# A three-sublayer decoder block: expert weights split in advance through a ring, base experts by groups of tiles, the step loop written out, and a causal zeroing on GpSimd

## The chip, the cores and the metric

The kernel runs on one core of one Trainium2 chip. The metric is the device time of one execution in microseconds (us), lower is better. Three timed runs of the kernel before gave 732.4, 735.15 and 735.88 us.

## The reference, cut to what matters

There are 16 sequences of 128 tokens with 256 features. Each sublayer adds its input and normalizes the rows afterwards.

```python
x = layernorm(x + self_attention(x))        # 16 heads of 16, one shared K/V head, causal, softmax
x = layernorm(x + cross_attention(x, ctx))  # 32 query heads on 8 K/V heads of 8, softmax
# mixture: a base expert for all tokens, and 2 of 8 experts (256 -> 2*512 -> 256) for each token
probs = softmax(x @ gate_w); w, idx = top_k(probs, 2); w = w / w.sum()
y = silu_mul(x @ base_gate_up) @ base_down
  + sum_e comb[:, e] * (silu_mul(x @ expert_gate_up[e]) @ expert_down[e])
x = layernorm(x + y)
```

All inputs and outputs are float32.

## The kernel before

There are two stages. The attention stage handles one sequence (one tile of 128 rows) per step in a software pipeline of 22 steps. Each engine has an order written by hand (`PE_ORDER`, `ACT_ORDER`, `DVE_ORDER`, `POOL_ORDER`, `SP_ORDER`); an entry such as `("s_main", 0, 2)` means that in step s the engine does unit 0 of that stage for tile s + 2. An engine runs its order strictly from left to right, and semaphores tie the engines together. Eight of the 22 steps run as two passes of a loop with four steps in its body (`run`), the others are written out.

In self-attention, scores are computed twice: with queries on partitions for the row maximum (`s_max`), and with keys on partitions, the maximum subtracted (`s_main`), for the exponential. ScalarE takes the exponential (`s_exp`, L438), and `s_sum` multiplies the weights with V and with ones. The causal mask is added by TensorE as a bf16 product with the identity, ahead of both score products:

```python
pe.matmul(scores[:, n, at:at + 512], ident_b[:], mask_kq[:], start=True, stop=False)      # L784
mm = pe.matmul(scores[:, n, at:at + 512], k_s[p][:, b, :], q_s[p][:, 4 * bank:4 * bank + 4, :], start=False, stop=True)
```

Score results go through a ring of two PSUM slots, smaller ones through the ring `misc` of two banks, exponentials through four slots of `prob`. Products that need the accuracy of float32 are written in the attention stage as three products of FP32R parts (`three`, L722: high times high, high times low, low times high). Float32 products in the expert stage are single instructions for the programmer, and stand in the trace as two records each.

The expert stage begins when the attention stage has ended. TensorE transposes the 16 tiles (L1251), computes the router logits (L1258), and then works through 55 jobs: 10 tiles of the base expert, 39 tiles of rows sorted by expert, and 6 base tiles. While the first base jobs run, VectorE works out which row goes where (`shift_logits` to `slot_rows`), and GpSimd then gathers rows by indirect DMA three jobs ahead. A job is two halves of inner products (512 columns each, L1299), four transposes of the hidden tile (`turn_hidden`, L1306), two transposes of a later job's rows (`turn_rows`, L1313) and the outer product (L1322). Before the first half of a sorted job the sequencer of TensorE waits for the turned rows, and then reads the expert's number from memory (`value_load`, L1292). All weights of the eight experts lie in SBUF. Each result tile is copied out and scattered to HBM. During the last base jobs the chosen results come back, and VectorE adds them with their shares (`add_shares`, L1182 and L1185), then the last normalization follows.

Of the kernel before, what the change touches and what calls it, by code (L numbers as in the profile page):

```python
# [7 lines left out]
F32 = mybir.dt.float32  # L8
F32R = mybir.dt.float32r
# [16 lines left out]
CONST_COLS = 3 * P + 22  # L26
# [7 lines left out]
BASE_FIRST = 10  # L34
AHEAD = 3
ROUTE_COLS = 2 * P + SLOTS + EXPERTS * EXPERTS + PICKS + 1 + EXPERTS
# [15 lines left out]
    ("s_shift", 0, 3), ("c_main", 3, 0), ("s_out", 1, 2), ("c_max", 1, 1), ("c_sum", 0, 0),  # L52
]
# [5 lines left out]
    ("c_exp", 3, 0), ("s_rows", 0, 4),  # L59
# [11 lines left out]
    ("s_split", 0, 4), ("c_keys", 0, 1), ("x_bias", 0, 2),  # L71
]
SP_ORDER = [
    ("load_xT", 0, 4), ("load_ctx", 0, 2), ("load_base", 0, 2), ("load_x", 0, 2),
]
# [22 lines left out]
    "c_out": [("c_ctx", 2, None)],  # L98
}
# [81 lines left out]
def decoder_layer(nc, x, xT, ctx, ctxT, wqkvT, bqkv, woT, bo, gate_w, base_gu, base_down, exp_gu, exp_down, consts,  # L181
                  routing, out):
    x2 = nc.dram_tensor("x2", (B * S, D), F32, kind="Internal").ap()
    shared = nc.dram_tensor("chosen_y", (CHOICES * B * S, D), F32, kind="Internal").ap()
    with ExitStack() as both:
# [6 lines left out]
        base_up, base_dn = sb("base_up", [P, 2, 2 * INNER]), sb("base_dn", [P, INNER // P, D])  # L192
        ident = sb("ident", [P, P])
        eps = sb("eps", [P, 1])
        gate = sb("gate", [P, 2, EXPERTS])
        base_loaded = both.enter_context(nc.semaphore("base_loaded"))
        attention(nc, x, xT, ctx, ctxT, wqkvT, bqkv, woT, bo, consts, stream, ident, eps, base_gu, base_down,
                  gate_w, gate, base_up, base_dn, base_loaded)
        experts(nc, exp_gu, exp_down, routing, x2, shared, stream, ident, eps, gate, base_up, base_dn, base_loaded, out)


def attention(nc, x, xT, ctx, ctxT, wqkvT, bqkv, woT, bo, consts, stream, ident, eps, base_gu, base_down,
              gate_w, gate, base_up, base_dn, base_loaded):
    score_ring, prob_ring, sum_ring, misc_ring = rings()
    with ExitStack() as scope:
# [3 lines left out]
        def two(name, shape, dt=F32):  # L209
# [10 lines left out]
        mask_qk, mask_kq = sb("mask_qk", [P, 4, P], BF16), sb("mask_kq", [P, 4, P], BF16)  # L220
        blk_s, blk_c = cst[:, 3 * P:3 * P + 2], cst[:, 3 * P + 2:3 * P + 6]
        neg_s, neg_c = cst[0:32, 3 * P + 6:3 * P + 14], cst[0:32, 3 * P + 14:3 * P + 22]
# [43 lines left out]
        names = """consts_loaded weights_loaded w_hi w_split wo_split tables values_set  # L266
            xT_hi_set xT_split x_biased s_qkv_full s_qkv_read s_rows_hi s_rows_lo s_q_full s_q_read s_k_full s_k_read
            s_max_full s_max_read s_shift_full s_shift_read s_main_full s_exp s_summed s_sum_read
            s_out_full s_den_set s_ctx s_ctx_full s_ctx_hi s_ctx_read s_res_full s_res_read s_stats s_mv s_ln s_rsqrt0
# [8 lines left out]

        wo_loaded = scope.enter_context(nc.semaphore("wo_loaded"))
# [4 lines left out]
        def run(eng, order, stages):  # L284
# [6 lines left out]
            for s in range(FIRST_STEP, LOOP_FROM):  # L291
                step(s)
            with eng.Fori(0, LOOP_STEPS // UNROLL) as i:
                for u in range(UNROLL):
                    step(LOOP_FROM + u, i)
            for s in range(LOOP_FROM + LOOP_STEPS, LAST_STEP + 1):
                step(s)
# [9 lines left out]
        def _(sp):  # L307
# [28 lines left out]
            def load_base(seq, unit):  # L336
                if seq.i is None and seq.off == 0:
                    sp.dma_start(base_up[:], base_gu.rearrange("(k p) n -> p k n", p=P)).then_inc(base_loaded, 16)
# [3 lines left out]
            run(sp, SP_ORDER, dict(load_xT=load_xT, load_x=load_x, load_ctx=load_ctx, load_base=load_base))  # L342

        @block.gpsimd
        def _(pool):

            for p in range(2):
# [8 lines left out]
            def s_split(seq, unit):  # L356
# [4 lines left out]
                if seq.i is None and seq.off == 0:  # L361
                    pool.wait_ge(sem["w_hi"], 2)
                    pool.tensor_tensor(wo_lo[:], raw_wo[:], f32(wo_hi[:]), ALU.subtract).then_inc(sem["wo_split"], 1)

# [21 lines left out]
            run(pool, POOL_ORDER, dict(s_split=s_split, x_bias=bias, c_keys=c_keys))  # L386

        @block.scalar
        def _(act):
# [109 lines left out]
            def c_turn(seq, unit):  # L499
                wait(act, sem["c_main_full"], seq.back(2), 4)  # L500
                for u in range(2):
# [4 lines left out]


# [8 lines left out]
                                     c_turn=c_turn, c_exp=c_exp, c_read=c_read, c_log=c_log, c_rsqrt=c_rsqrt))  # L516

        @block.vector
        def _(dve):
# [9 lines left out]
            dve.tensor_copy(mask_kq[:], cst[:, 2 * P:3 * P].unsqueeze(1).broadcast_to([P, 4, P]))  # L529
# [191 lines left out]
        def _(pe):  # L721
# [55 lines left out]
            def s_main(seq, b):  # L777
# [4 lines left out]
                for bank in range(2):  # L782
                    at = 512 * bank
                    pe.matmul(scores[:, n, at:at + 512], ident_b[:], mask_kq[:], start=True, stop=False)  # L784
                    mm = pe.matmul(scores[:, n, at:at + 512], k_s[p][:, b, :], q_s[p][:, 4 * bank:4 * bank + 4, :],  # L785
                                   start=False, stop=True)
# [75 lines left out]
            def c_sum(seq, unit):  # L862
# [7 lines left out]
                for v in range(2):  # L870
# [4 lines left out]

            pe.wait_ge(sem["w_split"], 1)
            run(pe, PE_ORDER, dict(s_qkv=s_qkv, s_turn=s_turn, s_max=s_max, s_shift=s_shift, s_main=s_main, s_sum=s_sum, s_out=s_out,
                         s_proj=s_proj, s_res=s_res, c_turn=c_turn, c_max=c_max, c_shift=c_shift, c_main=c_main,
                         c_sum=c_sum, c_out=c_out))

def experts(nc, exp_gu, exp_down, routing, x2, shared, stream, ident, eps, gate, base_up, base_dn, base_loaded, out):
    with ExitStack() as scope:  # L882
# [11 lines left out]
        pairs = inner[:].rearrange("p a b n -> p (a b) n")  # L894
# [7 lines left out]
        up = sb("up", [P, EXPERTS, 2, 2 * INNER])  # L902
        down = sb("down", [P, EXPERTS, INNER // P, D])
        cst = sb("route_cst", [P, ROUTE_COLS])
        at = 0
# [11 lines left out]
        xT = sb("router_xT", [P, 2, B * S])  # L917
        rows, sortedT = [sb(f"rows{p}", [P, D]) for p in range(AHEAD + 1)], two("sortedT", [P, 2, P])
        silu, hidden = two("silu", [P, INNER]), two("hidden", [P, INNER])
# [476 lines left out]
```

## Time and profile before

| | us |
|---|---|
| median of three runs (lowest, highest) | 735.15 (732.4, 735.88) |
| the profiled execution, its time | 725.34 |
| the profiled execution, its span | 723.5 |
| TensorE busy in it | 660.0 (91%) |
| VectorE, ScalarE, GpSimd busy | 383.3, 309.7, 135.3 |

A profile is one execution. Busy time of TensorE is not TensorE at its peak, because its matmuls overlap and their ends are modelled; the distance between the starts of neighbours says more. Views used are the page's slices, the windows, the timeline of an engine, the chain that ended last, and the list of one source line.

### The profile page before, as it was taken

The numbers are of one execution on the slowest core, as the hardware profiler recorded it, in microseconds if no ns is written. First come the engines' busy times: TensorE is split into PE (matmuls) and PEld (weight loads), VectorE is DVE, ScalarE is ACT, GpSimd is POOL, SyncE is SP. The second block draws the span as 40 slices with busy tenths as digits, with TensorE's granted clock in tenths as the row PEclk, the third lists the DMA queues.
The fourth block names the chain that finished last, engine by engine and source line by source line (L and its number), as shares of the span: only waits on it lengthen the run. The fifth ranks groups of instructions, "written<-read, shape, count | busy, mean of one in ns | idle before, by whom it ended". The sixth has DMA issues, their size and how long they took to land. (4 is left out here: it accounts for less than half of the span.)

```text
span 723.5 us, 10370 instructions
## 1 busy us (share of the span) xinstructions
PE 660.0 (91%) x3039; PEld 391.4 (54%) x3067; DVE 383.3 (53%) x884; ACT 309.7 (43%) x661; POOL 135.3 (19%) x155
## 2 busy tenths in 40 slices
PE   2778999999989999998679899999999999999991
PEld 2445555555545554543266566666666666666660
DVE  3568788898877888887625621111221211111286
ACT  2346666666656666665542112222222222222115
POOL 2011111111011111111000200233333333332100
PEclk9999999999999999999998999999999999999996
DMA  6100000000000000000049800011111111111343
GB/s 181 29 23 23 18 6 22 23 24 24 23 24 8 14 22 15 15 15 2 0 156 388 304 7 0 30 50 39 41 50 39 43 38 44 40 43 38 104 129 116
DMA packets 33073, 40.01 MB, mean 55 GB/s; under 512 B 5404, under 2 KB 28447, under 8 KB 33024
## 3 DMA queue, kind: packets, MB, share of 16 engines
q1 hardware_dynamic: 29280, 30.10, 12.8%
q0 software_dynamic: 3744, 9.31, 4.1%
q8 instruction: 24, 0.39, 0.2%
q14 instruction: 25, 0.20, 0.1%
HBM read 31.01 MB, written 9.31 MB: 56 GB/s over the span
## 5 line engine op out<-in xcount | busy, mean ns | idle before, releaser
L1299 PE MATMUL inner<-up,sortedT 128*128 x312 | 146.7, 592 | 0.0
L1162 DVE TENSOR_TENSOR hidden<-silu,inner 128x512 f32<-128x512 f32 x55 | 37.8, 686 | 170.8 <-PE inner L1299 170.1
L1039 ACT ACTIVATE silu<-inner 128x512 f32<-128x512 f32 x55 | 32.8, 597 | 191.6 <-PE inner L1299 191.6
L438 ACT ACTIVATE prob<-scores 128x1024 f32<-128x1024 f32 x96 | 98.3, 1026 | 11.5 <-PE scores L785 7.4
L565 DVE TENSOR_REDUCE max_c<-scores 128x8 f32<-128x1024 f32 x64 | 78.0, 1219 | 6.9 <-PE scores L848 5.8
L1299 PEld LDWEIGHTS inner<-up,sortedT 128*128 128x128 f32 x312 | 56.2, 190 | 39.4 <-issue 37.3
L1322 PE MATMUL y<-down,hT 128*128 x312 | 73.8, 379 | 0.0
L1015 POOL DMA_INDIRECT chosen_y<-y_rows,to_row x39 | 39.6, 1015 | 179.4 <-DVE y_rows L1173 175.5
L872 PE MATMUL sums<-prob,v_c 128*32 128x512 f32 x256 | 63.7, 621 | 0.0
L1299 PE MATMUL inner<-base_up,router_xT 128*128 128x512 f32 x128 | 61.4, 606 | 0.0
L1322 PEld LDWEIGHTS y<-down,hT 128*128 128x128 f32 x312 | 56.4, 190 | 7.0 <-issue 1.0
L360 POOL TENSOR_TENSOR xT_lo<-xT_in,xT_hi 128x256 fp32r<-128x256 f32 x16 | 12.0, 747 | 234.8 <-ACT xT_hi L409 234.8
L1008 POOL DMA_INDIRECT rows<-x,from_row x39 | 38.2, 980 | 82.0 <-DVE from_row L1156 70.4
L858 PE MATMUL scores<-q_c,k_c 128*128 128x512 f32 x128 | 46.0, 440 | 6.2 <-ACT prob L438 2.7
L848 PE MATMUL scores<-k_c,q_c 96*128 96x512 f32 x128 | 46.1, 442 | 3.8 <-DVE max_c L565 3.8
L565 DVE TENSOR_REDUCE max_s<-scores 128x8 f32<-128x1024 f32 x32 | 39.1, 1222 | 11.7 <-PE scores L761 11.7
L1306 PEld LDWEIGHTS hiddenT<-ident,hidden 128*128 128x128 f32 x220 | 27.5, 141 | 28.6 <-issue 28.3
L381 POOL TENSOR_TENSOR k_c<-k_split,cst 96x512 fp32r<-96x512 f32 x32 | 32.7, 1041 | 47.0 <-DVE k_split L674 47.0
L1173 DVE COPY y_rows<-y 128x256 f32<-128x256 f32 x39 | 16.6, 425 | 46.5 <-PE y L1322 46.5
L858 PEld LDWEIGHTS scores<-q_c,k_c 128*128 128x128 f32 x128 | 19.3, 190 | 33.1 <-issue 26.9
L1049 ACT COPY sortedT<-turned 128x256 f32<-128x256 f32 x39 | 14.5, 373 | 50.7 <-PE turned L1313 50.7
L761 PE MATMUL scores<-k_s,q_s 96*128 96x256 f32 x128 | 35.6, 391 | 0.0
(187 smaller groups left out, 1052.2 us busy)
## 6 DMA issues: line engine op xcount, KB each, us to landing
up<-in_exp_gu SPq DMA_DIRECT2D x8, 1024.0 KB, 13.3
down<-in_exp_down SPq DMA_DIRECT2D x8, 512.0 KB, 12.2
up<-chosen_y SPq DMA_DIRECT2D x8, 512.0 KB, 8.3
xT_in<-in_xT SPq DMA_DIRECT2D x16, 128.0 KB, 2.2
x_in<-in_x SPq DMA_DIRECT2D x16, 128.0 KB, 2.2
x<-stream SPq DMA_DIRECT2D x1, 2048.0 KB, 10.0
ctxT_in<-in_ctxT SPq DMA_DIRECT2D x16, 96.0 KB, 2.3
out<-stream SPq DMA_DIRECT2D x2, 768.0 KB, 3.7
```

Source lines behind the costliest of these rows:

```text
L438: act.activation(prob[:, m, :], scores[:, n, :], ACT.Exp, scale=scale).then_inc(sem[exped], 1)
L565: dve.tensor_reduce(out_[:, 8 * unit:8 * unit + 8], scores[:, n, :].rearrange("p (h k) -> p h k", k=S), AX.X, ALU.max).then_inc(sem[read], 1)
L761: mm = pe.matmul(scores[:, n, at + 256 * v:at + 256 * v + 256], q_s[p][0:96, 4 * unit + 2 * bank + v, :], k_s[p][0:96], start=False, stop= ...
L848: mm = pe.matmul(scores[:, n, 512 * v:512 * v + 512], q_c[p][0:96, 2 * unit + v, :], k_c[p][0:96, unit // 2], start=True, stop=True)
L858: mm = pe.matmul(scores[:, n, 512 * v:512 * v + 512], k_c[p][:, a, 2 * (unit % 2) + v, :], q_c[p][:, 4 * a:4 * a + 4, :], start=True, stop ...
L872: mm = pe.matmul(sums[32 * j:32 * j + 32, n, :], v_c[p][:, a, 32 * j:32 * j + 32], prob[:, m, 512 * v:512 * v + 512], start=True, stop=True)
L1008: pool.indirect_dma_start(out=rows[j % (AHEAD + 1)][:], out_offset=None, in_=x2, in_offset=bass.IndirectOffsetOnAxis(ap=from_row[:, j:j + ...
L1015: pool.indirect_dma_start(out=shared, out_offset=bass.IndirectOffsetOnAxis(ap=to_row[:, j:j + 1], axis=0), in_=y_rows[j % 3][:], in_offset ...
L1039: act.activation(silu[q % 2][:], inner[:, q % 2, 0, :], ACT.Silu).then_inc(sem["silu_set"], 1)
L1162: dve.tensor_tensor(hidden[q % 2][:], silu[q % 2][:], inner[:, q % 2, 1, :], ALU.mult).then_inc(sem["hidden_set"], 1)
L1299: mm = pe.matmul(inner[:, q % 2, h, :], tokens(q, k), w, start=(k == 0), stop=(k == 1))
L1322: mm = pe.matmul(y[:, 0:D], hT[q % 2][:, c, :], w, start=(c == 0), stop=(c == INNER // P - 1))
```

## The change

- **Causal zeroing.** `s_main` no longer adds the mask. After `s_exp`, GpSimd sets the weights with key later than query to zero by index (`s_causal`, an affine select in place on 128x1024), and `s_sum` waits for that instead of for the exponential.
- **Split in advance.** During the attention stage GpSimd splits each half of an expert's weights into a high and a low FP32R part (`w_high`, three `w_low`, 1,536 columns a step), SP loads the raw half and stores both parts to HBM. It also splits the base expert's input weights (`base_split`).
- **Loop written out.** The step loop is replaced by plain steps.
- **x2 in the attention stage.** Each finished tile is transposed (`x2_turn`), copied (`x2_read`) and stored (`store_x2`) there.
- **Ring.** The expert stage holds split weights of three experts; SP loads the next when the one three before is done.
- **Split products.** The inner products of base and experts, and the outer product of the experts, are FP32R products: six for a half, twelve for an outer product (the base expert's outer product stays float32). `half` reads two values (slot, and the count of experts to wait for).
- **Base by groups.** The base expert works on groups of four tiles with the weights stationary, in four chunks of 128 hidden columns, so its hidden tiles need no transposes. Two groups precede the 39 sorted tiles, two follow.

```diff
+    ("s_causal", 0, 2), ("s_split", 0, 4), ("w_high", 0, 2), ("c_keys", 0, 1), ("w_low", 0, 2), ("s_causal", 1, 2), ("w_low", 1, 2),
+    ("x_bias", 0, 2), ("w_low", 2, 2), ("base_split", 0, 2),
...
+                pool.affine_select(keys_first, keys_first, [[0, 8], [1, S]], ALU.is_ge, no_weight, base=0, channel_multiplier=-1)\
+                    .then_inc(sem["s_causal"], 1)
...
+                pool.tensor_copy(halves[p][:, 0, :], raw_w[p][:]).then_inc(sem["w_high"], 1)
...
+                pool.tensor_tensor(halves[p][:, 1, n * third:n * third + n], raw_w[p][:, n * third:n * third + n],
+                                   f32(halves[p][:, 0, n * third:n * third + n]), ALU.subtract).then_inc(sem["w_low"], 1)
...
-                    pe.matmul(scores[:, n, at:at + 512], ident_b[:], mask_kq[:], start=True, stop=False)
...
-                wait(pe, sem["s_exp"], seq, 2, b + 1)
+                wait(pe, sem["s_causal"], seq, 2, b + 1)
...
+                if h == 0:
+                    pe.wait_ge(sem["turned_hi"], j + 1)
+                    if j == 0:
+                        pe.wait_ge(sem["tile_set"], 1)
+                    slot_of[j] = pe.value_load(tile_slot[0:1, j:j + 1], min_val=0, max_val=RING - 1)
+                    needed = pe.value_load(tile_ready[0:1, j:j + 1], min_val=1, max_val=EXPERTS)
+                free_inner(u, h)
+                if h == 0:
+                    pe.wait_ge(sem["weights_ready"], needed)
...
+                for k in range(2):
+                    pe.matmul(into, sT_hi[j % 2][:, k, :], w(0, k), start=(k == 0), stop=False)
+                    pe.matmul(into, sT_hi[j % 2][:, k, :], w(1, k), start=False, stop=False)
...
+            for j in range(SORTED):
+                if j + 1 < SORTED:
+                    half(j + 1, 0)
...
+                turn_hidden(j)
+                if j + 1 < SORTED:
+                    half(j + 1, 1)
...
+                if j + 2 < SORTED:
+                    turn_rows(j + 2)
+                outer(j)
```

## Rows read from the trace of the kernel before

**Rows 1.** The page's 40 slices, busy tenths of TensorE

```profile
PE   2778999999989999998679899999999999999991
```

**Rows 2.** The page's chain that ended last, by line

```profile
PE inner L1299 26%; PE y L1322 13%; PE hiddenT L1306 3%; PE route L1258 1%; PE turned L1313 1%; ACT stream L1066 1%; PE inner L1251 1%; DVE stream L1182 0%; DVE stats L1185 0%; PE route L1273 0%; DVE mv L1198 0%; DVE stream L1170 0%; PE route L1267 0%; ACT lnv L1061 0%; ACTq L882 0%
```

**Rows 3.** Windows: stretch, length, busy us of each engine, clock, DMA

```profile
95.00:203.00 108.00, 105.94 (x568) 57.76 (x578) 90.66 (x214) 71.61 (x160) 20.51 (x24) 1.00 0.07 20
...
447.00:671.00 224.00, 224.00 (x848) 138.85 (x847) 42.96 (x77) 55.35 (x115) 71.85 (x72) 1.00 0.13 40
```

**Rows 4.** VectorE's timeline, once a step: start, us, line

```profile
201.56 0.41 DVE L668 TENSOR_SCALAR x<-pre,mv_s,t_s 128x256 f32<-128x256 f32 x1
...
225.67 0.41 DVE L668 TENSOR_SCALAR x<-pre,mv_s,t_s 128x256 f32<-128x256 f32 x1
...
245.56 0.41 DVE L668 TENSOR_SCALAR x<-pre,mv_s,t_s 128x256 f32<-128x256 f32 x1
```

**Rows 5.** Timeline, s_main(1) on TensorE

```profile
242.10 0.39 PE L784 MATMUL scores<-mask_kq,ident_b 128*128 128x512 bf16 x1
...
242.57 0.39 PE L784 MATMUL scores<-mask_kq,ident_b 128*128 128x512 bf16 x1
```

**Rows 6.** GpSimd's timeline, the elementwise operations it has

```profile
8.34 1.28 POOL L363 TENSOR_TENSOR wo_lo<-raw_wo,wo_hi 128x512 fp32r<-128x512 f32 x1
...
241.47 0.73 POOL L360 TENSOR_TENSOR xT_lo<-xT_in,xT_hi 128x256 fp32r<-128x256 f32 x1 [17.17 <-ACT xT_hi L409]
242.16 2.04 POOL L381 TENSOR_TENSOR k_c<-k_split,cst 96x512 fp32r<-96x512 f32 x2
```

**Rows 7.** Timeline of a step, what meets the new GpSimd work

```profile
227.58 0.49 DVE L679 TENSOR_TENSOR rows_c<-x,rows_c 128x128 fp32r<-128x128 f32 x2
...
231.37 0.41 DVE L706 TENSOR_TENSOR pre<-ctx_c,x 128x256 f32<-128x256 f32 x1
...
233.01 1.08 PE L796 MATMUL sums<-prob,v_s 128*64 128x512 f32 x4
...
239.89 1.03 ACT L438 ACTIVATE prob<-scores 128x1024 f32<-128x1024 f32 x1
```

**Rows 8.** Timeline of one sorted job

```profile
504.28 0.60 PE L1306 MATMUL hiddenT<-ident,hidden 128*128 128x128 f32 x4
...
506.44 0.38 PE L1313 MATMUL turned<-ident,rows 128*128 128x128 f32 x2
...
506.66 1.89 PE L1322 MATMUL y<-down,hT 128*128 x8
...
506.86 0.37 ACT L1049 COPY sortedT<-turned 128x256 f32<-128x256 f32 x1 [1.30 <-PE turned L1313]
...
508.38 1.88 PE L1299 MATMUL inner<-up,sortedT 128*128 x4
```

**Rows 9.** List of L1292 in 505.8 to 511.7, TensorE's sequencer: ns, start

```profile
L1292 PEldq TENSOR_LOAD <-tile_expert x1: 303/303/303, 507.3 to 507.3; - x1
...
L1292 PEldq SEQ_ASSERT  x1: 18/18/18, 507.8 to 507.8; - x1
```

**Rows 10.** Timeline of the routing, and the gathers' time to landing

```profile
370.17 5.33 PE L1251 MATMUL inner<-ident,stream 128*128 128x128 f32 x32 [3.94 <-PEq L205]
...
384.43 0.29 DVE L1090 TENSOR_REDUCE stat_max<-route 128x16 f32<-128x128 f32 x1 [8.98 <-PE route L1258]
...
397.02 4.43 DVE L1133 TENSOR_TENSOR lane_hot<-route_cst,place_lane 128x4096 bf16<-128x4096 f32 x1
...
DMA to landing us min/median/max: 2.6/2.8/3.8
```

**Rows 11.** Timeline of the end on VectorE

```profile
707.66 0.43 DVE L1185 BATCH_NORM_STATS2 stats<-stream 128x6 f32<-128x256 f32 x1
...
709.03 0.43 DVE L1185 BATCH_NORM_STATS2 stats<-stream 128x6 f32<-128x256 f32 x1
...
718.97 0.73 DVE L1215 TENSOR_SCALAR stream<-stream,mv,rstd 128x256 f32<-128x256 f32 x2
```

More of the change, by code:

```diff
@@ L98 @@
     "c_out": [("c_ctx", 2, None)],
+    "x2_turn": [("x2_read", 1, 1)],
 }
@@ L290, in step @@
                         stages[stage](seq, unit)
[L291 to L296, printed above, removed]
+            for s in range(FIRST_STEP, LAST_STEP + 1):
                 step(s)
@@ L384, in c_keys @@
                 ins.then_inc(sem["ctx_k_set"], 1)
-            run(pool, POOL_ORDER, dict(s_split=s_split, x_bias=bias, c_keys=c_keys))
+            run(pool, POOL_ORDER, dict(s_causal=s_causal, s_split=s_split, x_bias=bias, c_keys=c_keys, w_high=w_high, w_low=w_low,
+                                       base_split=split_base))
         @block.scalar
@@ L505, in c_turn, with x2_read @@
                         .then_inc(sem["c_q_read"], 1)
+            def x2_read(seq, unit):
+                n = misc_ring.slot("x2_turn", 0, seq)
+                wait(act, sem["x2_turned"], seq)
+                act.copy(xT2[:, :, S * seq.off:S * seq.off + S], misc[:, n, 0:2 * S].rearrange("p (k t) -> p k t", k=2))\
+                    .then_inc(sem["x2_read"], 1)
             act.preload_act_table_set("natural_log_exp_and_others")
@@ L874, in c_sum, with x2_turn @@
                 mm.then_inc(sem["c_summed"], 1)
+            def x2_turn(seq, unit):
+                n = misc_ring.slot("x2_turn", 0, seq)
+                wait(pe, sem["x2_set"], seq)
+                misc_ring.wait_free(pe, sem, "x2_turn", 0, seq)
+                for k in range(2):
+                    mm = pe.transpose(misc[:, n, S * k:S * k + S], stream[:, seq.off, P * k:P * k + P], ident[:])
+                mm.then_inc(sem["x2_turned"], 1)
             pe.wait_ge(sem["w_split"], 1)
@@ L967, in reach, with f32, y_bank @@
                 eng.wait_ge(s, v)
-        def sorted_before(q):
-            return sum(kind == "sorted" for kind, _ in jobs[:q])
-        def base_before(q):
-            return sum(kind == "base" for kind, _ in jobs[:q])
+        def f32(ap):
+            return ap.bitcast(F32)
+        def y_bank(o):
+            kind, n = outs[o]
+            return hiddenT[:, 0:2, :].rearrange("p a b -> p (a b)") if kind == "base" and n % 2 else y[:, 0:D]
         block = scope.enter_context(nc.Block())
@@ L1221, in _ @@
             choose_second()
[L1222 to L1237 removed]
+            multiply(1)
@@ new lines, in _ @@
+            group_low(1)
+            multiply(2)
+            place_picks()
+            multiply(3)
+            hot_lanes()
+            multiply(4)
+            take(0)
+            take(1)
+            hot_slots()
+            take(2)
+            take(3)
+            multiply(5)
+            tile_experts()
+            multiply(6)
+            slot_rows()
+            multiply(7)
+            turn_rows(0)
+            turn_rows(1)
+            for o in range(TILES, FIRST_OUTS):
+                take(o)
@@ new lines, in _ @@
+            u = use_of("base", GROUPS_FIRST, 1)
+            for m in range(CHUNKS):
+                multiply(u + m)
+            first = FIRST_OUTS + SORTED
+            later = [[0, 1], [2, 3], [4, 5], [6, 7]]
+            for m in range(TILES):
+                take(first + m)
+            for m in range(CHUNKS - 1):
+                for t in later[m]:
+                    add_shares(t)
+                multiply(u + CHUNKS + m)
+            for t in later[3]:
+                add_shares(t)
@@ L1238, in _ @@
+            for m in range(TILES):
+                take(first + TILES + m)
+                if m < 2:
+                    add_shares(8 + 2 * m)
+                    add_shares(9 + 2 * m)
+            variance(0)
+            add_shares(12)
             newton(0)
-            for t in range(NORM_PARTS[1][0], NORM_PARTS[1][1]):
+            for t in range(13, B):
                 add_shares(t)
@@ L1307, in turn_hidden @@
+            def turn_hidden(j):
+                pe.wait_ge(sem["hidden_set"], use_of("sorted", j) + 1)
+                reach(pe, sem["hT_lo"], j)
+                if j == 0:
+                    pe.wait_ge(sem["y_read"], FIRST_OUTS)
+                for c in range(CHUNKS):
+                    mm = pe.transpose(hiddenT[:, c, :], hidden[j % 2][:, P * c:P * c + P], ident[:])
                 mm.then_inc(sem["hT_full"], 1)
```

478 lines of the change are left out of this document (314 added, 164 removed).

## The prediction, on record before the changed kernel was seen

> **What bounds the kernel now.** I read the page's slices first, then the chain, then windows by stage, then the timelines. TensorE is at 9 tenths nearly everywhere [rows 1], and the chain of what ended last is TensorE in the expert stage, above all the inner products of L1299 (26% of the span) and the outer products of L1322 (13%) [rows 2]. In the sorted jobs its busy time fills the window completely, 224.0 of 224.0 us, at clock 1.00 [rows 3]: there the kernel is bound by the float32 products. A sorted job is 5.82 us. It can be read off as 1.71 us for a half (from the second half's start, right behind the four transposes), 0.43 us for those transposes, 0.22 us for two transposes of rows (506.44 to 506.66) and 1.72 us for the outer product (506.66 to 508.38) [rows 8]: 2 x 1.71 + 0.43 + 0.22 + 1.72 = 5.8.
>
> In attention the picture is another. A step is 20.2 us on average outside the loop's edge; TensorE shows 98% busy, VectorE 84%, ScalarE 66% and GpSimd 19% [rows 3]. Two consecutive marks at 201.56 and 225.67 are 24.1 us apart, the next 19.9 [rows 4]: the first pair spans the jump back of the loop, which costs 24.1 - 20.2 = 3.9 us.
>
> **The change part by part.** The sum is made against the profiled execution, 723.5 us of span and 725.34 us of time. That execution is 9.8 us (1.3%) below the median of the runs, so the difference is what I carry to the median 735.15.
>
> *Loop written out.* The jump's 3.9 us goes [rows 4], I add 0.6 for its entry (an estimate): -4.5 us.
>
> *Mask out of s_main.* Two mask products of 512 columns and two score products take 0.94 us a unit, two times 0.47 [rows 5]; half of that goes, so 0.94 us a step. x2_turn adds two transposes, 0.22 us [rows 8]. TensorE does 0.7 us less of 20.2. It gains less than that where it waits for VectorE's or ScalarE's reading of a score slot; bounds are 0 and 0.7, I take 0.4. x2_read on ScalarE costs 0.37 us, the price of the copy of turned rows [rows 8], and ScalarE is idle for a third of the step [rows 3]: hidden.
>
> *GpSimd.* Its subtraction with two inputs took 1.28 us for 512 columns and 0.73 for 256, so 2.1 ns a column and 0.2 us fixed [rows 6]. Per step the change adds three w_low at 1.28 (3.8 us), a cast of 1,536 columns and two affine selects of 1,024. Neither of the last two is in the trace. From above I bound them by the two-input price, 3.5 and 2.4 us; from below by 0.9 ns a column, less than half of it because there is one input and not two, 1.5 and 1.1 us (the lower end is an estimate; nothing shows less). I take 2.4 and 1.7. Together with what is there, 0.73 + 2.04 + 0.73 [rows 6], the step is 3.8 + 2.4 + 3.4 + 3.5 = 13.1 us (11.0 to 15.6) of 20.2: GpSimd stays below the step. What counts is when. s_exp(0) ends at 240.9 [rows 7]; behind it in strict order come the first select (to 242.6), s_split (243.3), w_high (245.7), c_keys (247.8), a w_low (249.1) and the second select (250.8). s_sum(1) starts at 233.01 in the previous step, so is due at 253.2 [rows 7]: 2.4 us of slack. The first s_sum has more. So the new waits cost nothing in steady steps, and without this cover, each us that the selects and the cast take together beyond 2.4 comes on top of each of 16 steps. In the filling steps there is no such cover, since TensorE has little else to do; I put 4 us there, twice the second select's wait behind w_high and w_low (bounds 0 and 8).
>
> *VectorE beside a busy GpSimd.* VectorE's operations with both inputs in SBUF, c_rows (two, 227.58, again at 247.8) and c_res (231.37, at 251.6) [rows 7], would now run while GpSimd reads SBUF. In the trace of before no such pair overlaps, since GpSimd is done at 244.9 (after its 0.73 of x_bias), so the price is bounded by 0 and by one whole GpSimd operation each, 3 x 1.28 = 3.8 us a step. I take 0.5 on the step, since c_rows and c_res have about 1 to 2 us before somebody needs them. The Trainium skill says more, in "SBUF — State Buffer", section "Who interferes with whom": such a VectorE instruction and a GpSimd one that reads SBUF exclude each other for the whole instruction. By it the bound of a whole operation is what happens; no row here shows it either way.
>
> So a steady step changes by -0.4 + 0.5 = +0.1 us; over 14 of them +1. Attention: -4.5 + 4 + 1 = about 0, with bounds of -16 (a gain of 0.7, no fill) and about +45.
>
> *Start of the experts.* The 32 transposes of 5.33 us [rows 10] go; instead the last tile's transpose, copy and semaphores take 1.2 us. -4.1 us. The loads of the first three experts (9.4 MB) have 50 us.
>
> *First base groups.* An FP32R product of 512 columns costs what is left of the 0.47 us pair, 0.235 [rows 5]; six make 1.41 us for a half, so a chunk 2.8 us. Eight chunks are 22.6 us, and a group's outer product is four float32 ones, 6.9 us [rows 8]. Counted from the end of the logits (384.3, [rows 10]): TensorE reaches the end of the second group's inner products at 35 us, of which 1.6 are a wait for the second choice, and 1.8 a wait because the take of the first result stands behind the 4.43 us of hot_lanes on VectorE [rows 10]. Rows are known at 34.6 (25.7 before; VectorE has seven multiplies, a 1.2 us group_low and four takes ahead of it), the first gather lands 2.8 us later [rows 10], TensorE waits 2.5 us, and turns, outer product and two halves end at 49.2.
>
> *Sorted jobs.* By TensorE's work alone a job would be 4 x 0.705 = 2.82, + 0.43 + 0.22 + 12 x 0.115 (the float32 product shows 0.108 for 256 columns in one pass, 1.72 / 16, and I add a little for weights) = 4.86 us. But the sequencer doesn't come that far. half(j + 2, 0) waits for turned rows, and they are copied 0.79 us after the transposes of rows begin (506.44 to 507.23) [rows 8]. Only then comes value_load: from 507.3 to 507.84 [rows 9], 0.6 us with its neighbours, and now there are two of them, 1.2 us; then 0.3 us until the first product can start. From the start of a job the transposes of rows begin at 1.41 + 0.44 + 1.41 = 3.26, so the next half starts at 3.26 + 0.79 + 1.2 + 0.1 + 0.3 = 5.65 us. Before, the same chain was 3.87 + 0.79 + 0.6 + 0.4 = 5.66 and lay just inside 5.82 [rows 8, 9]. Bounds are 4.86, if the loads overlap something, and 5.9. 37 jobs at 5.65 and two at 4.86 are 218.8 us, against 232.3 before for the same stretch (which then holds one more base job's half): most of what TensorE saves is idle time. ScalarE (1.6 us a job) and VectorE (2.2) stay far below.
>
> *Last groups and end.* Four chunks and an outer product are 18.2 us. VectorE adds a tile's shares every 1.37 us [rows 11]. Six tiles' shares and three multiplies put the last chunk's multiply at 11.05 us, so the last outer product runs from 11.2 to 19.2, with its third and fourth tile waiting for takes behind shares; four more tiles' shares, the norms, the scaling (0.73) and the last store follow as before [rows 11]: 34.8 us.
>
> Sum from the end of the logits: 49.2 + 218.8 + 18.2 + 34.8 = 321.0, before 723.5 - 384.3 = 339.2: -18.2. With -4.1 and 0: -22 to -23 us. 735.15 - 23 = 712.
>
> **Rivals.** (a) *The sequencer keeps up.* If value_load costs less beside the waits, a sorted job is 4.86: 37 x 0.79 = 29 us less, 683 us. For it speaks that 0.3 us of a value_load is the load itself [rows 9]; against it that everything in a sequencer is in order. (b) *Slower: GpSimd and VectorE exclude each other.* If each of the three two-input operations waits for a whole GpSimd operation, and VectorE (84% busy) has nothing to absorb it, a step grows by 3.8 - 0.4 = 3.4 and not by 0.1: 14 x 3.3 = 46 more, 758. From a step 1.7 us longer on the change is a loss (23 / 14 on top of 0.1). The skill's rule named above speaks for it. Against it: most of the wait is where c_turn and s_den are not yet due, so a step more like +2, 739 us. (c) *The selects or the cast are slow.* With selects of 4 us (1,024 columns at twice the two-input rate) the second one ends at 255.4, 2.2 us late: 16 x 2.2 = 35, 747 us. (d) *TensorE gives back nothing at all in the experts*, the job at 5.85 by a longer chain: +7, 719.
>
> **How the numbers follow.** Forecast with (d) inside its own bounds: 0.52. (a) 0.18. (b) 0.14. (c) 0.10. Something else in attention, as a fill that costs more: 0.06. The likeliest is 712. The range 680 to 746 takes in (a), the milder (b) and nearly (c). A measurement tells about 0.5%, 3.7 us. Faster is the forecast, (a) and a little of the rest: 0.73; same 0.07; slower 0.20.
>
> **What would show it.** A sorted job of 5.65 us with TensorE idle for 0.8 us before L1299's first product of each job and two loads of 0.5 us in the sequencer's list: right. Jobs of 4.9: (a). A select of 1.1 to 2.4 us and steps of 20 to 20.5: right; VectorE's c_rows or c_res longer or with idle time ahead while GpSimd works: (b); L796 waiting for GpSimd: (c). No 24 us step at the loop's edge. The wrongest number would be the attention step, since each 0.1 us in it is 1.5 us of time.

## The result, and the profile after

The changed kernel took 803.57 us (median of 4 runs, 800.75 to 804.63), the kernel before beside it 733.77 (4 runs, 724.33 to 735.88): ratio 1.0992, 95% interval 1.088 to 1.1104. It is 10% slower, where 712 us and a range up to 746 had been forecast. The profiled execution took 800.75 us, its span is 798.1 us.

The page of the changed kernel: 40 slices of TensorE and of its clock, and the chain by line.

```profile
PE   3766888877977789788778799889889888988982
...
PEclk9889998989989899899976769999999999999996
...
DMA rows<-x,from_row 5%; PE inner L1525 4%; PE inner L1530 3%; PE inner L1526 3%; PE y L1560 2%; PE y L1561 2%; PE y L1564 2%; PE route L1439 2%; PE y L1501 2%; PE hiddenT L1539 1%; PE inner L1479 1%; PE inner L1480 1%; PE inner L1484 1%; DVE stream L1327 1%; PE hiddenT L1501 1%
```

TensorE has fallen from 9 tenths to 7 and 8 in the attention stage [rows 1], and at the head of the chain, where the inner products were [rows 2], now stands a DMA, the gather of rows. Windows of the changed kernel (columns as in [rows 3]): steady steps, the logits, the sorted jobs.

```profile
95.00:203.00 108.00, 89.39 (x451) 53.90 (x452) 94.25 (x169) 59.33 (x131) 50.53 (x45) 0.89 0.32 108
...
451.30:465.10 13.80, 13.80 (x65) 13.80 (x66) 1.45 (x4) 1.04 (x1) 0.00 (x0) 0.50 0.96 389
...
517.00:733.00 216.00, 190.16 (x1104) 158.85 (x1103) 78.84 (x147) 54.56 (x112) 70.83 (x71) 1.00 0.31 114
```

In the same 108 us of steps VectorE is busier (94.25 against 90.66) although it begins fewer instructions (169 against 214) [rows 3]: its instructions got longer. That is the sign to look for when two engines shut each other out; it does not show as idle time.

Four marks divide the span (VectorE's scaling `x<-pre,mv_s,t_s` of the first and the last tile, its last `stream<-pre,mv_c,t_c`, and `stat_max`, which follows the logits):

| us | before | after | change |
|---|---|---|---|
| start to the first x | 42.8 | 42.7 | -0.1 |
| 15 steps, x to x (mean of one) | 300.0 (20.0) | 375.9 (25.1) | +75.9 |
| last x to the last stream | 26.6 | 31.0 | +4.3 |
| last stream to stat_max | 15.0 | 15.6 | +0.6 |
| stat_max to the end | 339.1 | 333.0 | -6.1 |

The loss is in the steps: +75.9 beside 74.6 us in all. The expert stage gained 6 us where 18 were forecast. One steady step, timeline of VectorE, GpSimd, ScalarE and TensorE in the changed kernel:

```profile
214.01 1.46 POOL L410 CAST halves<-raw_w 128x1536 fp32r<-128x1536 f32 x1
215.44 2.04 POOL L444 TENSOR_TENSOR k_c<-k_split,cst 96x512 fp32r<-96x512 f32 x2
...
216.15 0.20 DVE L722 TENSOR_SCALAR t_c<-t_c,r_c 128x1 f32<-128x1 f32 x1
216.27 3.53 DVE L725 SCALAR_TENSOR_TENSOR t_s<-t_s,r_s 128x1 f32<-128x1 f32 x1
...
217.44 1.27 POOL L415 TENSOR_TENSOR halves<-raw_w,halves 128x512 fp32r<-128x512 f32 x1
...
218.66 1.09 POOL L401 TENSOR_SCALAR_AFFINE_SELECT prob<-prob 128x1024 f32<-128x1024 f32 x1
219.72 1.26 POOL L415 TENSOR_TENSOR halves<-raw_w,halves 128x512 fp32r<-128x512 f32 x1
219.72 1.30 DVE L725 SCALAR_TENSOR_TENSOR t_c<-t_c,r_c 128x1 f32<-128x1 f32 x1
220.94 0.87 DVE L737 TENSOR_SCALAR x<-pre,mv_s,t_s 128x256 f32<-128x256 f32 x1
...
221.84 0.30 ACT L558 CAST rows_c<-x 128x128 fp32r<-128x128 f32 x1 [3.94 <-DVE x L737]
...
223.09 1.19 PE L926 MATMUL scores<-q_c,k_c 128*128 128x512 f32 x2 [3.71 <-DVE max_s L634]
```

A Newton step (the three of them refine the reciprocal root that the normalization of a row needs, t_s in self-attention and t_c in cross-attention) works on 128x1 numbers and takes 3.53 us here. It ends when the zeroing of 218.66 ends; the next, t_c, ends with the subtraction of 219.72, and x with the addition of x_bias that began at 220.94. ScalarE waits 3.94 us for x, and TensorE 3.71 us for the maximum max_s, which stands right behind x in VectorE's order. The list by line, of the kernel before and then of the changed one (count | busy, mean ns | idle before):

```profile
L668 DVE TENSOR_SCALAR x<-pre,mv_s,t_s 128x256 f32<-128x256 f32 x16 | 6.6, 413 | 0.2
L656 DVE SCALAR_TENSOR_TENSOR t_s<-t_s,r_s 128x1 f32<-128x1 f32 x16 | 2.9, 184 | 0.1
L656 DVE SCALAR_TENSOR_TENSOR t_c<-t_c,r_c 128x1 f32<-128x1 f32 x16 | 2.6, 160 | 0.1
```

```profile
L725 DVE SCALAR_TENSOR_TENSOR t_s<-t_s,r_s 128x1 f32<-128x1 f32 x16 | 49.3, 3083 | 0.1
L737 DVE TENSOR_SCALAR x<-pre,mv_s,t_s 128x256 f32<-128x256 f32 x16 | 18.7, 1167 | 0.1
L725 DVE SCALAR_TENSOR_TENSOR t_c<-t_c,r_c 128x1 f32<-128x1 f32 x16 | 16.2, 1011 | 0.1
L748 DVE TENSOR_TENSOR rows_c<-x,rows_c 128x128 fp32r<-128x128 f32 x32 | 10.3, 361 | 1.3 <-ACT rows_c L558 1.3
```

These grew by 46.4 (t_s), 12.1 (x), 13.6 (t_c) and 2.4 us (rows_c, from 7.9): 74.5 us together. That this is about the loss proves nothing by itself, since part of such growth can be hidden: in the first run below, x, rows_c and the two Newton steps are together about 61 us longer than before and the steps lose 42. c_res (L775) has 418 ns before and after.

### The profile page after: what moved, and what is told of

It is laid out like the page before. It is cut to its first block and busy times, and to the rows that moved or that the text cites. A ratio compares the mean times of both kernels' runs of the same rounds, so it can differ in the third digit from the quotient of the medians.

```text
span 798.1 us, 11212 instructions
## 1 busy us (share of the span) xinstructions
PE 648.5 (81%) x3315; PEld 451.5 (57%) x3315; DVE 502.2 (63%) x971; ACT 308.6 (39%) x657; POOL 258.9 (32%) x255
## 5 line engine op out<-in xcount | busy, mean ns | idle before, releaser
L401 POOL TENSOR_SCALAR_AFFINE_SELECT prob<-prob 128x1024 f32<-128x1024 f32 x32 | 35.0, 1093 | 207.5 <-ACT prob L502 207.5
L1303 DVE TENSOR_TENSOR hT<-hiddenT,hT 128x512 fp32r<-128x512 f32 x39 | 27.0, 692 | 111.7 <-ACT hT L1148 111.7
L1525 PE MATMUL inner<-weights,sT_hi 128*128 x156 | 68.7, 440 | 21.4 <-issue 21.4
L1526 PE MATMUL inner<-weights,sT_hi 128*128 x156 | 61.6, 395 | 0.0
L415 POOL TENSOR_TENSOR halves<-raw_w,halves 128x512 fp32r<-128x512 f32 x48 | 61.5, 1281 | 0.1
L725 DVE SCALAR_TENSOR_TENSOR t_s<-t_s,r_s 128x1 f32<-128x1 f32 x16 | 49.3, 3083 | 0.1
L1530 PE MATMUL inner<-weights,sT_lo 128*128 x156 | 49.0, 395 | 0.0
L1525 PEld LDWEIGHTS inner<-weights,sT_hi 128*128 128x128 f32 x156 | 29.3, 188 | 31.6 <-issue 28.7
L830 PE MATMUL scores<-k_s,q_s 96*128 96x256 f32 x128 | 46.1, 480 | 0.0
L1560 PE MATMUL y<-weights,hT 128*128 x156 | 42.4, 303 | 0.5 <-ACT hT L1148 0.5
L558 ACT CAST rows_c<-x 128x128 fp32r<-128x128 f32 x64 | 14.3, 294 | 65.6 <-DVE x L737 65.6
L1561 PE MATMUL y<-weights,hT 128*128 x156 | 39.1, 283 | 0.0
```

The lines of the kernel that those rows point to most:

```text
L415: pool.tensor_tensor(halves[p][:, 1, n * third:n * third + n], raw_w[p][:, n * third:n * third + n], f32(halves[p][:, 0, n * third:n * thi ...
L725: dve.scalar_tensor_tensor(t[:, 2:3], t[:, 1:2], 1.5, r[:], ALU.add, ALU.mult).then_inc(done, 1)
L1525: pe.matmul(into, sT_hi[j % 2][:, k, :], w(0, k), start=(k == 0), stop=False)
L1526: pe.matmul(into, sT_hi[j % 2][:, k, :], w(1, k), start=False, stop=False)
L1530: mm = pe.matmul(into, sT_lo[j % 2][:, k, :], w(0, k), start=False, stop=(k == 1))
L1560: pe.matmul(into, hT[:, j % 2, 0, P * c:P * c + P], w(0, c), start=(c == 0), stop=False)
```

## The experiments

Each is compared with runs of the kernel before on the same chip (their medians 727 to 730 us), so ratios are what to compare.

**One wait removed.** The third Newton step as a tensor_scalar whose second operand is a pointer, in the changed kernel:

```diff
-                    dve.scalar_tensor_tensor(t[:, 2:3], t[:, 1:2], 1.5, r[:], ALU.add, ALU.mult).then_inc(done, 1)
+                    dve.tensor_scalar(t[:, 2:3], t[:, 1:2], 1.5, r[:], ALU.add, ALU.mult).then_inc(done, 1)
```

> The changed kernel, with the third Newton step written as a tensor_scalar with a pointer operand and not as a scalar_tensor_tensor with two tensors from SBUF; same arithmetic. Theory L (two-tensor operations of VectorE wait until GpSimd's backlog is done, and only they): the 3.53 and 1.30 us of the two last Newton steps fall to about 0.2, a step goes from 25.5 to 20 to 21 us, 725 to 735 us in all. Rival M (any VectorE operation from SBUF to SBUF of this stage waits, as the 4.39 us of the normalization L737 in one filling step suggests): the wait moves to L737, which then takes about 4 us, and the time stays at 795 to 805. Rival D (the weights' transfers or the zeroing's wait slow attention): unchanged as well, but with no long VectorE operation.

Measured: 765.1 us, ratio 1.0475 (1.0412 to 1.0538), a step 22.8 us. Its list by line:

```profile
L737 DVE TENSOR_SCALAR x<-pre,mv_s,t_s 128x256 f32<-128x256 f32 x16 | 48.1, 3004 | 0.1
L748 DVE TENSOR_TENSOR rows_c<-x,rows_c 128x128 fp32r<-128x128 f32 x32 | 26.4, 863 | 0.6 <-ACT rows_c L558 0.6
...
L725 DVE TENSOR_SCALAR t_s<-t_s,r_s 128x1 f32<-128x1 f32 x16 | 3.4, 211 | 0.1
```

The Newton steps are back at 0.2 us, and the wait of 3 us has moved to x, the next instruction that can be shut out. The time falls about half way, to neither theory's figure: most of the wait only changed its place. What is saved, as far as one step shows it, is that t_s, t_c and x no longer wait one after the other: from the start of the third Newton step to the end of x it is 3.7 us (204.32 to 207.99) where it was 5.5 (216.27 to 221.81).

**The mask back on TensorE**, in the changed kernel without the zeroing on GpSimd (two parts of the edit; `s_causal` is also taken out of `POOL_ORDER`):

```diff
+                    pe.matmul(scores[:, n, at:at + 512], ident_b[:], mask_kq[:], start=True, stop=False)
...
-                wait(pe, sem["s_causal"], seq, 2, b + 1)
+                wait(pe, sem["s_exp"], seq, 2, b + 1)
```

> The changed kernel, with the mask added by TensorE again and no zeroing on GpSimd. Theory L: GpSimd's dense stretch is 2.2 us shorter, so the Newton step waits about 2 us less in each of 16 steps, TensorE does 0.94 us more: 16 x 1 to 2 us, 770 to 790 us. If the zeroing's own wait for GpSimd were the cause, steps fall back to 20 to 21 us, 725 to 735. If it is the split alone, no change: 800.

Measured: 768.98 us, ratio 1.055 (1.0491 to 1.061), a step 22.7 us, t_s 1.62 us on average, t_c 0.95, x 1.08. With 2.2 us less of GpSimd's work in the stretch nearly half of the loss goes, though TensorE has 0.94 us more to do (768.98 lies 1 us below theory L's 770 to 790).

**The splitting moved.** The same work, but behind x_bias in GpSimd's order, where VectorE has mostly PSUM reads:

```diff
-    ("s_causal", 0, 2), ("s_split", 0, 4), ("w_high", 0, 2), ("c_keys", 0, 1), ("w_low", 0, 2), ("s_causal", 1, 2), ("w_low", 1, 2),
-    ("x_bias", 0, 2), ("w_low", 2, 2), ("base_split", 0, 2),
+    ("s_causal", 0, 2), ("s_split", 0, 4), ("c_keys", 0, 1), ("s_causal", 1, 2), ("x_bias", 0, 2),
+    ("w_high", 0, 2), ("w_low", 0, 2), ("w_low", 1, 2), ("w_low", 2, 2), ("base_split", 0, 2),
...
+                wait(pool, sem["c_res"], seq.back(3))
```

> The changed kernel, with the split of the expert weights moved behind x_bias in GpSimd's order and held until the residual add of cross-attention (c_res) of the same step, so that its 5.3 us lie where VectorE has no two-tensor operation. GpSimd's work is the same. Theory L: the last two Newton steps together wait 1.6 us at most and not 4.8, c_rows and c_res not at all; a step of 20.5 to 22 us, 725 to 750 us. Rival D (traffic or the amount of GpSimd's work): 795 to 805.

Measured: 732.49 us (10 runs), ratio 1.0059 (1.0022 to 1.0095). Steady steps are 19.8 to 20.1 us, and the last stream comes at 380.48 against 449.53. Two rows of its list:

```profile
L726 DVE SCALAR_TENSOR_TENSOR t_s<-t_s,r_s 128x1 f32<-128x1 f32 x16 | 13.5, 842 | 0.1
L738 DVE TENSOR_SCALAR x<-pre,mv_s,t_s 128x256 f32<-128x256 f32 x16 | 13.0, 815 | 0.1
```

In the window 200 to 300 us GpSimd is busy for 53.75 us, against 42.52 in the same window of the changed kernel, and TensorE's granted clock is 1.00 where it was 0.91. The weights are moved as before, so rival D falls. So neither the amount of GpSimd's work nor the prices of its instructions made the loss, but which of VectorE's instructions they met. The first five steps (22.1, 21.2, 23.2, 24.0 and 20.5 us, 12.8 us more than the same five before) take back more than the 5.7 us that the later ones gain, and the jobs are still as in the changed kernel.

**The zeroing alone, and the loop alone**, both from the kernel before: the step loop written out, and in the first of them the select on GpSimd too.

```diff
-            with eng.Fori(0, LOOP_STEPS // UNROLL) as i:
-                for u in range(UNROLL):
-                    step(LOOP_FROM + u, i)
...
+            for s in range(FIRST_STEP, LAST_STEP + 1):
+                step(s)
```

> The kernel before, with its loop written out and the causal zeroing on GpSimd, and nothing else of the change. GpSimd has 5.7 us of work in a step, 2.2 of it new. Forecast: -4.5 us for the loop, and 0 to -0.5 us a step from TensorE, less a wait of VectorE of up to 2 us where the zeroing meets a Newton step: 715 to 745, most likely 725 as far as the runs of before are 734.

> The kernel before with its step loop written out and nothing else changed. The prediction's step: the pass around the loop's edge (24.1 us against 20.2) goes, -4.5 us, so 724 to 727 beside 729.5 for the kernel before, ratio 0.992 to 0.996. Rival: longer code costs as much as the loop's edges did, ratio 0.998 or more. Beside the run with the zeroing as well (0.9868, 95% 0.9795 to 0.9942) it tells what the zeroing alone is worth: 0.4 to 0.7 us a step, 6 to 11 us.

Measured: with the zeroing 722.18 us, ratio 0.9868 (0.9795 to 0.9942), steady steps 19.5 to 19.6; the loop alone 727.07 us (10 runs), ratio 0.9969 (0.9934 to 1.0005), steady steps 20.2 to 20.3 and none of 24.1 [rows 4]. The loop's edge was worth 2.5 us of 4.5 by the medians, which cannot be told from nothing; in the two profiles the 15 steps take 295.6 us against 300.0, 4.4 less. The zeroing gives 0.7 us a steady step, of the 0.94 that TensorE has less to do in this run. In the whole time that is a ratio of 0.9868 / 0.9969 = 0.990, with intervals that touch, so the gain of the zeroing alone is shown for the steps and not for the whole. In its profile the steps are 5.6 us shorter than with the loop alone, but from the last x to stat_max it is 6.8 us longer (47.9 against 41.2), at a granted clock of 0.75 and then 0.59 where the other has 0.94 and 0.77.

**Both numbers read early**, in the changed kernel:

```diff
+            def read_values(j):
+                slot_of[j] = pe.value_load(tile_slot[0:1, j:j + 1], min_val=0, max_val=RING - 1)
+                needed_of[j] = pe.value_load(tile_ready[0:1, j:j + 1], min_val=1, max_val=EXPERTS)
...
                 turn_hidden(j)
+                if j + 2 < SORTED:
+                    read_values(j + 2)
```

> The changed kernel, but both numbers of sorted job j+2 are read by TensorE's sequencer right behind turn_hidden(j), while the queue of TensorE still holds work, not ahead of half(j+2, 0). Theory V (the two reads bound the job at 5.70 us, since they stand where the queue runs dry): the job falls to between 4.85 and 5.1 us, the pauses of 0.58 to 0.74 us ahead of the first half go, and the time falls by 37 x 0.6 to 0.85 = 22 to 31 us against the changed kernel, ratio to the kernel before 1.057 to 1.072. Rival U (the products themselves bound the job, or a read stops the engine wherever it stands): the job stays above 5.55 us and the time within 5 us of the changed kernel's.

**Gathers four jobs ahead**, in the changed kernel:

```diff
-AHEAD = 3
+AHEAD = 4
```

> The changed kernel with the gathers four sorted jobs ahead in place of three. Theory G (TensorE waits some 11 us in all for gathers that land up to 8.9 us after their issue while 3 MB weight loads run): those waits go, and the time falls by 7 to 11 us against the changed kernel, ratio to the kernel before 1.083 to 1.092. Rival H (a gather that is late because the queue is full of the weight load is as late when it is issued 5.7 us earlier, because it then still stands behind the same load): the waits for rows stay above 8 us in all, and the time stays within 3 us.

Measured: reads early 785.98 us, ratio 1.076 (1.0682 to 1.0838); gathers early 792.6 us, ratio 1.0859 (1.0792 to 1.0927). In the changed kernel TensorE pauses ahead of the first product of nearly every sorted job for nothing that the profile shows (issue), and the five long gathers stand in its chain, each issued 2.6 us behind the issue of a 3 MB weight load (by SP, at 555.06, 579.25, 608.76, 632.54 and 656.78). Timeline of the changed kernel, then its chain in order of time:

```profile
597.87 0.49 PE L1525 MATMUL inner<-weights,sT_hi 128*128 x1 [0.54 <-issue]
...
602.36 0.63 PE L1564 MATMUL y<-weights,hT 128*128 x4
603.58 0.50 PE L1525 MATMUL inner<-weights,sT_hi 128*128 x1 [0.58 <-issue]
```

```profile
557.62 8.15 DMA rows<-x,from_row
...
659.34 8.87 DMA rows<-x,from_row
```

With the reads early the job is 4.87 us in place of 5.69, but five jobs then take 7.5 to 11.3 us. The waits of TensorE for the gathers, with the reads early and with the gathers early:

```profile
PE turned L1550 <- DMA rows<-x,from_row: 19.7, 7, 4.2
```

```profile
PE inner L1525 <- issue: 20.1, 36, 0.7
...
PE turned L1546 <- DMA rows<-x,from_row: 2.4, 1, 2.4
```

From the first turn_hidden to the last, 38 jobs, it is 223.7 us in the changed kernel, 211.7 with the reads early (the five late gathers cost 24.8 over the period, against 7.2), and 216.4 with the gathers early. The pause was thus that of the two reads. Theory V held for the job and missed the sum, -17.6 where -22 to -31 was expected: a faster job outran its rows. Theory G held (11 us less by the medians, 10 by the ratios): a gather still takes up to 9.1 us to land, but is issued one job earlier.

**All cures together**, and the same without the Newton edit:

> The changed kernel with all the cures: the splitting of the weights behind x_bias in GpSimd's order, the third step of both Newton iterations with one input and a pointer, the two reads of job j+2 behind turn_hidden(j), the gathers four jobs ahead. If the costs are separate they add up: 732.5 (the splitting late) less 22 to 31 (reads) less 7 to 11 (gathers) less 0 to 10 (Newton) is 680 to 703, ratio to the kernel before 0.935 to 0.965. If one hides behind another (a faster job waits for its weights or its rows), it is 703 to 722, and the waits for weights_ready or rows on TensorE show it.

> The run with all the cures, but the third step of both Newton iterations as it was (scalar_tensor_tensor). If the Newton step matters no longer once the splitting stands late (its wait is 0.85 us a step there, off or partly on the path): within 5 us of the run with all the cures, 688 to 695, ratio 0.943 to 0.953. If it does, 15 steps x 0.4 to 0.7 us more: 696 to 700, ratio 0.953 to 0.96.

Measured: 689.62 us, ratio 0.9465 (0.9405 to 0.9525), 5.4% faster than the kernel before; without the Newton edit 694.57 us, ratio 0.9529 (0.9453 to 0.9605). The 38 jobs take 187.1 us, 4.92 each; no wait for weights or rows is left on TensorE. stat_max to the end is 296.8 us in both. So the two cures of the jobs, 12 and 7 us alone, are worth 37 together (187.1 against 223.7), because a faster job alone waits more for its rows. The expected 680 to 703 us was met. The Newton edit is worth 5.4 us by the last stream (380.99 against 375.60), 4.0 of it in the first two steps (22.5 and 21.2 us against 20.4 and 19.3) and none in the steady ones; the medians differ by 5.0, just inside the 5 us of the first expectation, and the intervals overlap. With all cures the steady steps are 19.8 us; two of 24 are left, in which GpSimd also splits the base expert's weights.

**The exclusion by itself.** Thirty instructions of VectorE, ten kinds, beside unbroken stretches of GpSimd:

> Not the decoder block: a kernel by itself, whose output is zeros and whose time stands for nothing. VectorE runs the same thirty instructions (ten kinds, three of each) five times: alone, and beside an unbroken stretch of GpSimd of zeroings (128x1024), of subtractions (128x512, two inputs), of casts (128x1536, one input), and of all three mixed. Theory P (it is the form of VectorE's instruction that decides, whatever GpSimd runs): the tensor_scalar with two pointers, the tensor_tensor and the scalar_tensor_tensor with both inputs in SBUF, the 128x1 ones too, last 1 to 4 us each beside GpSimd, each until the end of some instruction of GpSimd; those with numbers in place of pointers, copies, reductions and those that read PSUM keep their time alone within 10%. Rival Q (GpSimd's kind decides as well: only its two-input subtractions shut VectorE out, or only its zeroings): one or two of the stretches show no waits. Rival R (any VectorE instruction on SBUF waits): copies and reductions from SBUF wait too.

The list of VectorE by shape, alone:

```profile
L118 DVE TENSOR_TENSOR tiles<-src,big 128x256 f32<-128x256 f32 x3 | 1.1, 410 | 0.0
L120 DVE TENSOR_TENSOR tiles<-scores,src 128x256 f32<-128x256 f32 x3 | 1.1, 406 | 0.0
...
L126 DVE TENSOR_REDUCE small<-src 128x1 f32<-128x256 f32 x3 | 1.1, 398 | 0.0
...
L116 DVE COPY tiles<-src 128x256 f32<-128x256 f32 x3 | 0.7, 279 | 0.0
L108 DVE TENSOR_SCALAR small<-a,r 128x1 f32<-128x1 f32 x3 | 0.5, 206 | 0.0
L110 DVE SCALAR_TENSOR_TENSOR small<-a,r 128x1 f32<-128x1 f32 x3 | 0.3, 148 | 0.0
```

and, from another window of the same list, beside zeroings of 1.09 us each:

```profile
L118 DVE TENSOR_TENSOR tiles<-src,big 128x256 f32<-128x256 f32 x3 | 3.8, 1302 | 0.0
...
L116 DVE COPY tiles<-src 128x256 f32<-128x256 f32 x3 | 3.4, 1171 | 0.0
...
L110 DVE SCALAR_TENSOR_TENSOR small<-a,r 128x1 f32<-128x1 f32 x3 | 1.8, 645 | 0.0
L120 DVE TENSOR_TENSOR tiles<-scores,src 128x256 f32<-128x256 f32 x3 | 1.1, 408 | 0.0
...
L126 DVE TENSOR_REDUCE small<-src 128x1 f32<-128x256 f32 x3 | 1.1, 401 | 0.0
L108 DVE TENSOR_SCALAR small<-a,r 128x1 f32<-128x1 f32 x3 | 0.5, 208 | 1.4 <-POOLq L84 1.4
```

All three kinds of GpSimd do it: the copy takes 1.17 us beside zeroings, 1.35 beside subtractions and 1.55 beside casts, each about the length of one GpSimd instruction. Rival Q falls. Theory P is right on the two-input forms and on PSUM, and wrong on copies and on tensor_scalar with numbers (280 ns alone, 1169 beside zeroings), which wait too when 128x256 from SBUF to SBUF. R is wrong on reductions. A tensor_scalar of 128x1 is not shut out.

**Why 3.5 us, and not one instruction's length?**

> Not the decoder block: a kernel by itself, whose output is zeros and whose time stands for nothing. GpSimd runs the changed kernel's order of one step (zeroing, subtraction of 256 columns, cast of 1536, the pair of key products on 96 partitions, subtraction, zeroing, subtraction, subtraction of 256, subtraction), and VectorE beside it the query product, the three Newton steps of both normalizations, the scaling of 128x256 and a maximum, three times in each of four forms: as in the changed kernel; with the Newton steps not chained by semaphores; with a semaphore between the two key products; with two subtractions in place of the key products. Asked is why the first waiting instruction of a step lasts 3.5 us in the changed kernel and no waiting instruction beside a plain stretch of GpSimd lasted over 1.68 us. Theory K (the unbroken pair of key products takes VectorE's turn): the first form shows 3 us or more, the third and fourth at most 1.7. Theory S (the chain of semaphores makes it lose its turn): the second form alone shows at most 1.7. Theory O (something else of the decoder block, such as TensorE's or ScalarE's work beside it): all four show at most 1.7.

Its timeline in the first form, and in the third:

```profile
13.54 1.76 DVE L147 SCALAR_TENSOR_TENSOR t_s<-t_s,r 128x1 f32<-128x1 f32 x1
...
15.33 1.32 DVE L151 TENSOR_SCALAR tile<-src,mv,t_s 128x256 f32<-128x256 f32 x1
...
77.76 2.04 POOL L82 TENSOR_TENSOR key_out<-keys,blocks 96x512 fp32r<-96x512 f32 x2
...
78.06 0.76 DVE L147 SCALAR_TENSOR_TENSOR t_s<-t_s,r 128x1 f32<-128x1 f32 x1
...
78.85 4.59 DVE L151 TENSOR_SCALAR tile<-src,mv,t_s 128x256 f32<-128x256 f32 x1
...
79.76 1.26 POOL L75 TENSOR_TENSOR low<-raw,high 128x512 fp32r<-128x512 f32 x1
80.97 1.09 POOL L71 TENSOR_SCALAR_AFFINE_SELECT prob<-prob 128x1024 f32<-128x1024 f32 x1
82.03 1.26 POOL L75 TENSOR_TENSOR low<-raw,high 128x512 fp32r<-128x512 f32 x1
```

All three theories fail. The pair of key products without a semaphore between them is waited for whole (1.76 us), but longer waits came only with the semaphore between: there x lasts 4.59 us, passed over at the ends of three GpSimd instructions (79.80, 81.02, 82.06) and let in with the fourth, the same in each of three repeats, with TensorE and ScalarE at rest. In the changed kernel t_s is passed over three times too (216.5, 217.5, 218.7). The second and fourth form show at most 1.75. So one wait can last several instructions of GpSimd, and one semaphore between two of them, which also lets t_s through after 0.76 us, was enough to change which instruction waits and for how long. The 3.53 us of t_s did not come again in the form with the changed kernel's order, and what gives VectorE its turn stays open.

## Why the prediction was wrong, point by point

- *VectorE beside a busy GpSimd* is the step that failed: it was put at +0.5 us a step, with a bound of 3.8, and the step as a whole at +0.1. Measured, the step as a whole grew by 5.1 us (20.0 to 25.1), and by 5.7 against the kernel before with the loop written out and the zeroing (290.0 us for the 15 steps, 19.3 each). It failed twice. Of VectorE's instructions it listed only c_rows and c_res; c_res lost nothing, c_rows 2.4 us in all. The third Newton step, a scalar_tensor_tensor with both inputs in SBUF, and s_ln (x) were overlooked, though they stand in `DVE_ORDER` where w_high, c_keys and w_low run on GpSimd, and feed the whole of cross-attention. They carry 72 of the 74.5 us by which the listed instructions grew. And its bound of one GpSimd instruction for each wait is no bound: t_s waits 3.53, x in the kernel by itself 4.59. The run with the splitting moved (ratio 1.0059 in place of 1.0992) shows that the meeting is the cause. The rule cited in the prediction, the Trainium skill's "SBUF — State Buffer", section "Who interferes with whom", holds here as to who shuts out whom; it also says that copies and tensor_scalar in a two-port mode take part and reductions on this chip never, as the lists above show (279 to 1171 ns, 398 to 401). Its wait of one whole instruction is what the unbroken stretches of one kind show, and not what t_s and x show, where the measurement decides. Had the whole `DVE_ORDER` been gone through and not two names, t_s, t_c and x would have come up too; three more waits of 1.28 us are 3.8 us a step (an estimate from the price in the prediction), above the 1.7 us from which it called the change a loss.
- *"No row here shows it either way"*: the trace of the kernel before does hold one such meeting, in its first tile. There the third Newton step takes 0.58 us, where its 16 have a mean of 0.18, and ends at 42.76 with GpSimd's x_bias (42.74):

```profile
42.01 0.73 POOL L372 TENSOR_TENSOR x_bias<-x_in,b_o 128x256 f32<-128x256 f32 x1
...
42.17 0.58 DVE L656 SCALAR_TENSOR_TENSOR t_s<-t_s,r_s 128x1 f32<-128x1 f32 x1
```

- *Rival (b)* was this mechanism with 758 us and 14 in 100, too low in both: 3.4 us a step for 5.1, and the expert stage's gain taken at full. The range ended at 746, below this rival's own figure.
- *Mask out of s_main*: right in size. The zeroing alone gives 0.7 of 0.94 us a step, without x2_turn; with it, and the splitting out of the way, steady steps are 19.8 us where the loop written out has 20.2 to 20.3, which is the 0.4 of the sum.
- *GpSimd*: select 1.09 us and cast 1.48, at the lower bounds of 1.1 and 1.5. No s_sum waits for GpSimd in a steady step; rival (c) is out. Of the 4 us for the filling steps nothing shows ahead of the first x (42.7 us, 42.8 before).
- *Loop written out*: the 24.1 us step is gone; 4.4 of the 4.5 us by the steps in the profiles, 2.5 by the medians.
- *Start of the experts*: -4.1 forecast, +0.6 measured. The transposes did go, but the 64 logit products take 13.8 us at a granted clock of 0.50, the level of 1.2 GHz, behind 2.66 us in which TensorE waits for the last stream. The stretch ahead of it, from the last x to the last stream, was not forecast to change and is 4.3 us longer, at a clock of 0.78 where it was 0.94. Before, the stretch of the logits took 9.0 us at 0.78, as this window of the kernel before shows:

```profile
375.30:384.30 9.00, 9.00 (x67) 9.00 (x65) 0.15 (x1) 1.03 (x3) 0.00 (x0) 0.78 1.03 355
```

- *First base groups*: the stretch ends at 515.8, where 49.2 us behind the logits would be 514.3.
- *Sorted jobs*: 5.65 forecast, 5.69 measured, and the pause is the sequencer's (the run with the reads early: 4.87). The whole stretch is 228.4 us for 218.8. Rival (a)'s job exists, but has to be written. What the step left out is the 7.2 us of late gathers: the loads of 3 MB were said to have room on the queues, which they have, and nobody asked what stands behind them.
- *Last groups and end*: 53.9 us for 18.2 + 34.8 = 53.0. The sum from the logits is 333.0 for 321.0: 1.5 us in the first groups, 9.6 in the sorted jobs, of which 7.2 are the gathers, and 0.9 here.

## What to carry to other kernels

Before work is put on GpSimd, go through VectorE's whole order in that stretch, down to its 128x1 instructions, and mark every one that has two inputs in SBUF or copies or scales from SBUF to SBUF; then place GpSimd's work where VectorE reads PSUM with at most one input from SBUF, or reduces. Price a meeting at several of GpSimd's instructions, not one, if the result is waited for. A small transfer issued shortly behind a large one can be late, and a pause removed can be given back there: cure both before judging either.

## What the runs showed of the hardware that was not expected

- A scalar_tensor_tensor of 128x1 (0.15 us alone) lasts up to 3.85 us beside GpSimd; a tensor_scalar of 128x1 stays at 0.21.
- A waiting VectorE instruction can be passed over at the ends of three GpSimd instructions (4.59 us in all), repeatably.
- TensorE's granted clock is 0.89 in the steps of the changed kernel, in which it waits more (busy 89.39 of 108 us), and 1.00 where the splitting stands late. How much of the 5.1 us a step the clock makes was not separated from the waits.
- A gather that lands in 2.8 us at the median takes 7.7 to 8.9 when it is issued 2.6 us behind a load of 3 MB.
- Two value_loads at the head of a job cost TensorE 0.82 us (5.69 to 4.87), and no pause when they are issued while TensorE's queue still holds work.
